# First batch's keys prepared in the latent-query stage, rows loaded in four pieces, four weights loaded in the fold's block

## The reference, cut to what matters

```python
q_hk = (hidden_q @ Wq.T).reshape(Bv, Sv, H, K)
q_big = jnp.einsum('bshk,hkq->bshq', q_hk, w_kc_q)
q_big = _apply_rope(q_big, sin_q[None, :, None, :], cos_q[None, :, None, :])
kv_r = _apply_rope(kv_c, sin_k[None], cos_k[None])
q_r = jnp.einsum('bshq,hqr->bhsr', q_big, W_qr)
k_r = jnp.einsum('bld,hdr->bhlr', kv_r, W_kr)
scores = jnp.einsum('bhsr,bhlr->bhsl', q_r, k_r)
attn = jax.nn.softmax(scores, axis=-1)
ctx_c = jnp.einsum('bhsl,bld->bhsd', attn, kv_r)
ctx_lat = jnp.einsum('bhsd,hkd->bhsk', ctx_c, w_kc_kv)
return ctx_lat.transpose(0, 2, 1, 3).reshape(Bv, Sv, H * K) @ Wo.T
```

## Time and profile before

| | us |
|---|---|
| median of 3 runs | 1923.76 |
| lowest and highest run | 1922.48, 1926.23 |
| the profiled execution | 1918.94 |
| its span | 1917.2 |
| PE busy | 1667.9 (87% of the span) |
| DVE busy | 1296.3 (68%) |
| POOL busy | 920.6 (48%) |
| ACT busy | 763.0 (40%) |

### The profile page before, as it was taken

How to read it: one execution, slowest core, us unless ns; L and a number is a source line. 1 busy time by engine, 2 the same in 40 slices (tenths; PEclk the granted TensorE clock), 3 DMA queues, 4 the chain that set the end, 5 groups by cost and what they waited for, 6 DMA issues and landing times. The chain is left out here.

```text
span 1917.2 us, 29070 instructions
## 1 busy us (share of the span) xinstructions
PE 1667.9 (87%) x9602; PEld 1165.1 (61%) x9602; DVE 1296.3 (68%) x2393; ACT 763.0 (40%) x1996; POOL 920.6 (48%) x815
## 2 busy tenths in 40 slices
PE   4999953999999999999999995799999379978890
PEld 3677731555555555555555553699999266654780
DVE  4577769777777777777777744587877666665333
ACT  2100000444444444444444452466666156642220
POOL 0366633777777777777788450223322000000536
PEclk9999975899999999999999997699999699988895
DMA  6133352122221122222221002666664340001343
GB/s 189 34 69 69 69 146 91 66 74 75 75 75 65 54 71 75 75 74 75 75 75 36 10 10 57 193 191 201 201 192 141 117 92 0 0 4 35 103 119 103
DMA packets 91670, 166.50 MB, mean 87 GB/s; under 512 B 45635, under 2 KB 70439, under 8 KB 86735
## 3 DMA queue, kind: packets, MB, share of 16 engines
q1 hardware_dynamic: 83727, 145.77, 25.7%
q0 software_dynamic: 7808, 19.02, 3.8%
HBM read 134.91 MB, written 29.53 MB: 86 GB/s over the span
## 5 line engine op out<-in xcount | busy, mean ns | idle before, releaser
L610 DVE TENSOR_REDUCE PM<-banks 128x2 f32<-128x964 f32 x320 | 360.9, 1133 | 139.5 <-PE banks L587 139.4
L802 ACT ACTIVATE R<-banks 128x400 f32<-128x400 f32 x768 | 326.7, 509 | 318.9 <-PE banks L837 318.0
L648 POOL TENSOR_TENSOR EA<-EA,R 128x400 f32<-128x400 f32 x288 | 306.6, 1064 | 121.3 <-ACT R L802 107.6
L847 PE MATMUL banks<-R,KV 128*64 128x400 f32 x1536 | 299.8, 512 | 0.0
L837 PE MATMUL banks<-QS,KH 128*128 128x400 f32 x768 | 289.4, 377 | 2.4 <-DMA QB<-ML 2.4
L837 PE MATMUL banks<-QB,KB 128*128 128x400 f32 x768 | 266.1, 346 | 0.0
L587 PE MATMUL banks<-KH,QS 64*128 64x482 f32 x320 | 161.0, 504 | 53.4 <-DVE KB L539 46.2
L628 DVE TENSOR_TENSOR banks<-banks,R 128x400 f32<-128x400 f32 x320 | 183.8, 574 | 27.8 <-ACT R L802 26.7
L175 PE MATMUL banks<-e_xh,e_split 128*116 128x256 f32 x960 | 194.4, 286 | 3.9 <-DVE e_xl L1622 3.9
L380 POOL TENSOR_TENSOR rotated<-rope_prod 96x400 f32<-96x400 f32 x128 | 131.7, 1049 | 133.7 <-DVE rope_prod L357 133.5
L587 PEld LDWEIGHTS banks<-KH,QS 64*128 64x128 f32 x320 | 60.8, 190 | 196.8 <-issue 107.7
(11 more groups left out here) (282 smaller groups left out, 3343.6 us busy)
## 6 DMA issues: line engine op xcount, KB each, us to landing
m_stage_u<-in_m_up SPq DMA_DIRECT2D x20, 1392.0 KB, 18.4
raw<-in_ctx_T SPq DMA_DIRECT2D x16, 1444.0 KB, 6.2
m_stage_d<-in_m_down SPq DMA_DIRECT2D x20, 696.0 KB
QS<-queries SPq DMA_DIRECT2D x16, 800.0 KB, 6.8
queries<-q_out_h SPq DMA_DIRECT2D x64, 100.0 KB, 2.4
queries<-q_out_l SPq DMA_DIRECT2D x64, 100.0 KB, 2.4
QB<-queries SPq DMA_DIRECT2D x16, 400.0 KB, 8.3
RS<-recips SPq DMA_DIRECT2D x32, 200.0 KB
```

Of the source, the lines that this page charges most:

```text
L610: nc.vector.tensor_reduce(PM[:, 2 * i:2 * i + n], banks[:, k:k + n, 0:KW], AX.X, ALU.max).then_inc(red_done, 1)
L648: nc.gpsimd.tensor_tensor(out, first, tile_of(n, 1), ALU.add).then_inc(odd_sum, 1)
L802: nc.scalar.activation(tile_of(n, o), psum[ring_bank(score_tile(b, n, o))][:, 0:CH], ACT.Exp).then_inc(exp_done, 1)
L847: last = nc.tensor.matmul(psum[CTX][o * DC:(o + 1) * DC, 0:CH], KV[b_mod(b)][:, t, :], tile_of(n, o), start=t == 0, stop=t == KT - 1)
```

## The change

One large buffer, arena (16384 columns), is held for the whole first attention. It first holds the six fold weights; once the fold is done the same place holds raw, rawk, prodk, the rope tables, KV of slot 0, and the latent stage's prod and rot, later the attention's CU, SU, RS, CT and ES. With that:

- The first block is gone. X is loaded in four pieces of four batches, each with its semaphore, then the identity, wq and wkq; DVE's statistics wait piece by piece. XN is a ring of 8 batches: groups 2 and 3 wait for the transposes of groups 0 and 1.
- wqr, wkr, wo and wkv are issued at the head of the fold's block.
- The latent stage's zeros tile has one batch, repeated by the DMA's source pattern. SP loads batch 0's keys and the rope tables there, and batch 0's queries ahead of the stores of c = 2. DVE does the constants of slot 0 and the rotation of batch 0 in pieces, one behind each second head. ACT copies KH at positions 20 and 21.
- At the head of the attention SP loads batch 1's keys and queries, then copies rows 0 to 63 of QB and KB from slot 0 into slots 1 and 2. DVE clears only the ends of slots 1 and 2.

```diff
 class FoldInputs:
@@ load
         sp.dma_start(self.wkq[:], dram["w_kc_q"].rearrange("h k q -> k h q")).then_inc(self.in_q, 16)
+
+    def load_more(self, sp):
         sp.dma_start(self.wqr[:], dram["W_qrT"]).then_inc(self.in_r, 16)
...
@@ layernorm, DVE
                 for b in range(known, B):
+                    if arrive and b % CB == 0:
+                        v.wait_ge(arrive[b // CB], 16)
                     core.batch_stats(X, b).then_inc(dve, 1)
...
                 for b in range(B):
+                    if b >= ring and b % CB == 0:
+                        v.wait_ge(turned, ((b - ring) // CB + 1) * KD)
...
+class LatentKeys:
...
+    def end_pads(self, ops, r):
+        ops.memset(as_f32(self.QS[r][:, H * S:]), 0.0)
+        ops.memset(as_f32(self.QB[r][DC:, H * S:]), 0.0)
+        ops.memset(as_f32(self.KH[r][:, SK:]), 0.0)
+        return ops.memset(as_f32(self.KB[r][DC:, SK:]), 0.0)
...
+    def first_batch(self, v, slot):
+        vec, QB, KB = self.core.nc.vector, self.QB[0], self.KB[0]
+        if slot == 1:
+            vec.memset(as_f32(QB[0:DC, :]), 0.0).then_inc(self.rows_set, 1)
+        elif slot == 2:
+            vec.memset(as_f32(KB[0:DC, :]), 0.0).then_inc(self.rows_set, 1)
...
+        elif slot == 6:
+            self.end_pads(vec, 0).then_inc(self.pads, 1)
+        elif 8 <= slot < 8 + self.ROT - 1:
+            if slot == 8:
+                v.wait_ge(self.consts, 32)
+            self.rotate_part(v, vec, 0, slot - 8)
+        elif slot in (23, 25):
+            self.rotate_part(v, vec, 0, self.ROT - 1 + (slot - 23) // 2)
...
@@ latent_queries, SP
+                keys.key_loads(sp, 0)
+                keys.rope_loads(sp)
...
                 for c in range(NC):
+                    if c == 2:
+                        for s in sent:
+                            sp.wait_ge(s, 16 + 64 * HP // SLOTS)
+                        keys.query_loads(sp, queries, 0, 0)
...
@@ latent_queries, DVE, behind each head
+                        if h % 2:
+                            keys.first_batch(v, c * HP + h // 2)
...
@@ latent_queries, ACT
+                        if c * HP + j in keys.HIGH_AT:
+                            keys.keys_high(act, 0, keys.HIGH_AT.index(c * HP + j))
...
@@ latent_attention, SP
-                key_loads(sp, 0)
-                sp.dma_start(ropeT[:], dram["rope_T"]).then_inc(consts, 16)
-                sp.dma_start(ropek[:], dram["rope_k"]).then_inc(consts, 16)
-                sp.wait_ge(pads, BUFS)
-                query_loads(sp, 0, 0)
-                query_loads(sp, 1, 1)
-                sp.wait_ge(k_ready, 1)
-                key_loads(sp, 1)
+                keys.key_loads(sp, 1)
+                keys.query_loads(sp, queries, 1, 1)
+                for r in range(1, BUFS):
+                    sp.dma_start(as_f32(QB[r][0:DC, :]), as_f32(QB[0][0:DC, :])).then_inc(rows_in, 16)
+                    sp.dma_start(as_f32(KB[r][0:DC, :]), as_f32(KB[0][0:DC, :])).then_inc(rows_in, 16)
+                sp.wait_ge(rows_in, 64)
                 max_rows(sp, 0, 0)
```

More of the change, by code:

```diff
@@ L80, in as_f32, with layernorm @@
     return ap.bitcast(F32)
-def layernorm(core, tag, X, XN, ident, XH, XL, known=0, loads=None, first=None):
+def layernorm(core, tag, X, XN, ident, XH, XL, known=0, loads=None, first=None, arrive=None, ident_in=None):
     nc, psum = core.nc, core.psum
+    ring = XN.shape[1]
     with ExitStack() as ctx:
@@ L217, in fold_weights, with _ @@
     with nc.Block() as block:
+        @block.sync
+        def _(sp):
+            w.load_more(sp)
         @block.tensor
@@ L267, in latent_queries @@
+def latent_queries(core, dram, XH, XL, AH, AL, M2, queries, normed, keys):
     nc, psum = core.nc, core.psum
@@ L296, in _ @@
                 for rows in normed:
-                    sp.dma_start(rows.rearrange("(b p) d -> p b d", p=Dispatch.PITCH)[S:], zeros[:]).then_inc(cleared, 16)
+                    sp.dma_start(rows.rearrange("(b p) d -> p b d", p=Dispatch.PITCH)[S:],
+                                 zeros[:].to_broadcast([Dispatch.PITCH - S, B, D])).then_inc(cleared, 16)
+                keys.key_loads(sp, 0)
+                keys.rope_loads(sp)
                 for s in sent:
@@ L776, in _ @@
                 act.sem_inc(cu_done, 1)
-                act.wait_ge(pads, BUFS)
-                for part in range(2):
-                    keys_high(act, FIRST, part)
                 max_high(act, FIRST)
@@ L853, in step @@
                         if has_next and m == 0:
+                            if b is FIRST:
+                                pe.wait_ge(pads, keys.PADS_FIRST + BUFS - 1)
+                                pe.wait_ge(rows_in, 64)
                             pe.wait_ge(k_ready, b_val(b) + 2)
@@ L2311, in model @@
         ident = fixed(ctx, nc, "ident", [P, P])
-        loaded = core.sem("loaded")
+        rows_in = [core.sem(f"rows_in{c}") for c in range(NC)]
+        ident_in = core.sem("ident_in")
         queries = nc.dram_tensor("queries", (B, P, H, S), F32).ap()
@@ L2316, in model, with first_loads @@
         results = [nc.dram_tensor(f"results{i}", (RESULTS, D), F32).ap() for i in range(2)]
-        with nc.Block() as block:
-            @block.sync
-            def _(sp):
-                sp.dma_start(X[:], dram["x"].rearrange("b s d -> s b d")).then_inc(loaded, 16)
-                sp.dma_start(ident[:], dram["ident"]).then_inc(loaded, 16)
-                sp.wait_ge(loaded, 32)
         with ExitStack() as layer:
             BB = fixed(layer, nc, "BB", [P, H // 2, D])
+            arena = fixed(layer, nc, "arena", [P, ARENA])
+            weights = FoldInputs(core, dram, arena)
+            keys = LatentKeys(core, layer, dram, arena)
+            def first_loads(sp):
+                rows = dram["x"].rearrange("b s d -> s b d")
+                for c in range(NC):
+                    sp.dma_start(X[:, c * CB:(c + 1) * CB], rows[:, c * CB:(c + 1) * CB]).then_inc(rows_in[c], 16)
+                sp.dma_start(ident[:], dram["ident"]).then_inc(ident_in, 16)
+                weights.load(sp)
             with ExitStack() as stage:
@@ L2333, in model @@
                 with ExitStack() as norm:
[L2334 to L2339 removed]
+                    XN = fixed(norm, nc, "XN_a", [S, 2 * CB, D])
+                    layernorm(core, "ln0_", X, XN, ident, XH, XL, 0, first_loads, None, rows_in, ident_in)
+                fold_weights(core, weights, AH, AL, M2, BB)
+                latent_queries(core, dram, XH, XL, AH, AL, M2, queries, normed, keys)
+            latent_attention(core, X, ident, queries, recips, BB, keys)
         core.release()
```

245 lines of the change are left out of this document (130 added, 115 removed).

## The result

| us | before | changed |
|---|---|---|
| median | 1924.89 (4 runs) | 1880.14 (4 runs) |
| lowest and highest | 1922.48, 1926.23 | 1875.82, 1884.27 |
| the profiled execution | 1918.94 | 1884.27 |
| its span | 1917.2 | 1882.5 |
| PE, DVE busy | 87%, 68% | 89%, 68% |

The ratio is 0.9769, 95% interval 0.9744 to 0.9793: 44.8 us off. Two later comparisons of the same pair gave 1925.34 to 1887.63 (0.9809, 0.9772 to 0.9846) and 1921.70 to 1884.22 (0.9807, 0.9782 to 0.9832), 37.7 and 37.5 us. The mean of the three is 40.0; the forecast was 41.0.

The account below looks back on a forecast made before the run. PE's own work was taken to bound nearly all, except holes at the start and the attention's head, DVE's stage. -5.1 + 0.4 + 0 - 36.3 = -41.0 us, from the median 1923.76 to 1882.8 us; range 1877 to 1892.

Parts of the forecast that it names:

- The statistics behind the pieces, -5.1 + 0.4: Start: only the last piece's four statistics follow X's landing, ending at 14.2 instead of 19.3, -5.1; XN's wait, +0.4.
- the ring: Start: XN's ring of 8 makes its third group wait for the first group's transposes, +0.4 us.
- X's last landing: Start: last piece of X taken to land at 12.9, between 12.2 and 13.5.
- Rival (b): The start gives nothing, as weights behind X slow it or come late: -36.3, 1887 us; (a), (b), (c) together 0.25.
- The weights, 0: Fold: four weights issued in its block land by 41.5, before its second half at 45.4; cover 3.9 us, cost nothing.
- The latent stage, 0: Latent queries: work inserted on DVE costs PE nothing, up to 3.0 us per insertion; 0 us, bounds 0 and +4.
- Rival (c): Latent queries: DVE and POOL exclude each other more, each rotate part holding PE 0.4: 1888 us; (a), (b), (c) together 0.25.
- The head, -36.3: Start of the attention: with nine short memsets left on DVE, the 20 maxima end 36.3 us earlier, at 297.0.
- Batch 1's keys: Attention's head: loads issued at 274.2 land in 6.8 us, POOL ends at 296.6, PE goes on at 300.5, 36.3 earlier.
- The copies: Attention's head: four row copies, 1.64 MB, end at 289 at 380 GB/s, wanted at 298.2; no cost, bound +3.5.
- Rival (a): Attention's head: copies land 3.5 us late and PE waits near 302: -37.5, 1886 us; (a), (b), (c) together 0.25.
- The other stages "as they are": All stages that the change does not touch: taken to keep their times, adding nothing to the sum.

Follow-up runs that it names:

- the experiment shows: Changed kernel with wqr, wkr, wo and wkv issued at the start behind wq and wkq, instead of in the fold's block: 1885.41 us, one run.
- By the experiment: Changed kernel with batch 0's rotation back at the head of the attention, short memsets and row copies kept: 1892.93 us.
- the row of insertions: Changed kernel with five extra DVE reductions of 2.74 us at latent-stage places 18 to 22, one behind each pair of heads: 1884.04 us, one run.

## Why the prediction was right

By its own steps:

- **The statistics behind the pieces, -5.1 + 0.4.** The fold starts 6.0 us earlier (31.91 to 25.90), where the sum had 4.7. The last statistics end 6.3 earlier (19.28 to 13.00), the ring costs 0.6, and 0.3 comes from the block's end, which SP's sixth weight no longer holds. The step was mis-sized in one term: X's last landing, taken at 12.9 from the end of traffic in before, came at 11.6, outside the 12.2 that I gave as its bound. The identity stood behind X in that traffic, but it is no explanation: it has 64 KB of 1.7 MB, and it too landed earlier (11.75, and 13.64 with X in one load). The four pieces moved at 231 GB/s where the one load moved at 179, which no row of before could show. Rival (b), weights behind X that slow it, did not come: X came sooner with them in the queue. Right: four of sixteen statistics behind the last piece (1.41 us), and the ring.
- **The weights, 0.** Right, and the cover as told: the fold's second half begins 17.5 behind the first with no wait. What the prediction did not see is why the four had to be moved: not for bandwidth, but because SP's last issue would hold the block to 28.9. It treated the start's -5.1 as the pieces' work alone; the experiment shows 3.5 to 4.0 of it to hang on this edit.
- **The latent stage, 0.** Right: 204.2 after 204.4, and 174.81 in both for the pairs that hold the insertions. The stated reason was too generous. "An insertion of up to 3.0 us costs PE nothing" holds for one alone and fails for a row of them, which lost 3.5 us at 2.74 each. The rotate parts came out at up to 1.38, not the 0.96 taken from the earlier trace rows; the smaller bound of 1.6 still covers them, and the number stands on that. Rival (c), 0.4 for each rotate part, did not come: the parts lengthen each other and POOL's additions, but stay within the idle time. The earlier trace rows showed that exclusion and it is there: 0.82 became 1.29, 2.06 became 3.00. The section "Who interferes with whom" of "SBUF — State Buffer" in the Trainium skill, by which the later of the two waits for the whole of the first, is borne out on POOL: the part begins 0.23 before the first addition's end (117.60 + 1.03), the second addition begins behind it, and the pair takes 0.94 longer. On DVE it gives 0.23 + 0.82 = 1.05, an estimate, where 1.29 was measured; the other 0.24 is not explained.
- **The head, -36.3.** Measured -36.2 (62.40 to 26.20), in parts: 1.5 for the memsets where I had 1.8, 20.96 for the maxima, KB 24.3 into the block where I had 24.5. By the experiment the rotation is 11.3 of it and the memsets, which the copies replace, 24.9.
- **Batch 1's keys**: POOL started 8.0 after the issue (6.8 taken) and ended 23.6 into the block (22.4). The 1.2 us were covered by the 2.1 between POOL's end and KB's turn; what remained was 0.8.
- **The copies**, which had no row before: they moved at 207 GB/s with all 16 engines' time used (share 1.00), where the loads before them ran at 364 to 411 (the DMA histogram of 260 to 320 us). I took 380 and reckoned their end at 15 us into the block; their traffic ended at 18.5 and the last had landed by 19.8. The figure of the Trainium skill's "SBUF — State Buffer", section "Door 1: The DMA port swizzle" (196 GB/s for partitions 0 to 63, at 1 MiB), cited in the prediction beside the sum, agrees with 207 and was nearer than the value that I chose. By either value the copies are in before the 24.0 at which they are wanted, so the number did not suffer. Rival (a), rows 3.5 late, would have needed copies some 8 us later than they came; made 9.9 later they cost 3.5.
- **The other stages "as they are".** Their code is, their time is not: the expert stage has 359.8 to 369.7 in fourteen profiles. That spread is larger than the distance of the three measured differences, -44.8, -37.7 and -37.5, from the forecast -41.0, so how near a single one of them came is luck; what the forecast can be held to is the part that the change touches, -41.5 at the end of the first attention. Whether the change shifts the mean of that stage by 1 to 3 us (its two profiles before have a mean of 362.6, the twelve after 365.5) cannot be told from two profiles and stays open.

## What to carry to other kernels

Look for the stage in which PE does nothing, sum what its own engine does there, and move all of it that depends on nothing near into another stage's idle time; here that was worth 36 of 42 us, and reading the sum from rows gave it within 0.1. For inserted work keep two numbers apart: the idle time per round, which can be spent every round, and the slack of the buffers, which can be spent once. And a block ends with its slowest queue: a DMA that nobody needs yet, or a store that nobody reads yet, still holds every engine until it has been issued or has landed (3.5 to 4.0 us at the fold, 4.4 at the end of the latent queries).

## What the runs showed of the hardware, beyond what was expected

- The issue of one DMA on SP is not a fixed cost. The load of wkv took SP 5.1 to 6.3 us with three weights issued just ahead of it (eleven profiles), 7.9 and 8.1 behind five weights in the kernel before, and 11.36 behind X and five weights; SP issues nothing else meanwhile. In the same way wkq took 1.7 to 2.1 us behind wq alone, and 5.8 to 7.0 behind X, the identity and wq.
- X in four loads moved at 231 GB/s in 3 to 7 us, in one load at 179, both at a DMA share of 0.70.
- Copies inside SBUF of 64 partitions took about twice the engine time per byte of loads from DRAM: 207 GB/s at a share of 1.00 in 277 to 285 us, where the loads ahead of them moved at 396 with a share of 0.98 (269.5 to 275 us).
- Three waits of 2.05 and 2.06 us in an otherwise full stretch of PE were each followed by some ten matmuls 0.33 us apart, at 1.2 GHz, which cost 1.55 us each time. Behind waits of 1.84 and 1.83 us, and behind four of up to 0.7 us in the row of insertions, the granted clock stayed at 1.00.
- An instruction of DVE with two SBUF inputs and POOL's additions hold each other up though they touch different columns: +0.47 us on a 128x722 part (0.82 to 1.29) and +0.94 us on POOL's pair (2.06 to 3.00).
